# Two attention and mixture-of-experts layers: layer-norm statistics spread over attention steps, token normalisation on GpSimd, three more batches masked by TensorE

## What is computed

```python
x = x + attn_a(LN(x))   # 16 heads of 8, causal mask, softmax(q k / sqrt(8))
x = x + ffn(LN(x))      # top 2 of 8 experts per token, silu(x Wg) * (x Wu) @ Wd
x = x + attn_b(LN(x))   # 16 heads of 8, no mask, per-head shift and scale from norms of q, k and x
x = x + ffn(LN(x))      # the same weights as the first ffn
```

## Time and profile before

| | |
|---|---|
| median of three runs | 1166.69 us (1163.05 to 1168.38) |
| the profiled execution's own time, and its span | 1166.68 us, 1164.9 us |
| TensorE matmul, weight load | 1029.9 us busy (88%), 716.6 us (62%) |
| VectorE | 755.5 us (65%) |
| ScalarE | 672.4 us (58%) |
| GpSimd | 525.5 us (45%) |
| chain that ended last | TensorE 60%, VectorE 11%, issue 6%, GpSimd 5%, DMA 4% |
| granted TensorE clock over the span | 0.92 |

### The profile page before, as it was taken

How to read it: one execution, slowest core, us unless ns; L and a number is a source line. 1 busy time by engine, 2 the same in 40 slices (tenths; PEclk the granted TensorE clock), 3 DMA queues, 4 the chain that set the end, 5 groups by cost and what they waited for, 6 DMA issues and landing times.

```text
span 1164.9 us, 28879 instructions
## 1 busy us (share of the span) xinstructions
PE 1029.9 (88%) x9290; PEld 716.6 (62%) x9290; DVE 755.5 (65%) x2322; ACT 672.4 (58%) x1399; POOL 525.5 (45%) x980
## 2 busy tenths in 40 slices
PE   2998999897989999999798979999888799999990
PEld 1444555453468989999443434444443589999990
DVE  4687778877777333456777888888877663334442
ACT  2365676663644545556277858897757445455550
POOL 2243444332742610344687736455736436004455
PEclk9998999996989999999778979998888899999995
DMA  6446544562235878887544323343221469778873
GB/s 152 104 114 138 116 110 99 151 181 57 54 118 174 271 233 236 260 255 236 125 111 104 101 56 85 89 107 84 65 49 44 130 191 280 227 242 256 272 225 109
DMA packets 201723, 175.03 MB, mean 150 GB/s; under 512 B 19812, under 2 KB 160616, under 8 KB 201576
## 3 DMA queue, kind: packets, MB, share of 16 engines
q1 hardware_dynamic: 193384, 156.41, 49.1%
q0 software_dynamic: 8192, 16.79, 4.8%
HBM read 122.99 MB, written 50.14 MB: 149 GB/s over the span
## 4 chain that ended last, share of the span: by engine, by line
PE 60%; DVE 11%; issue 6%; POOL 5%; DMA 4%; SPq 3%; ACT 1%; POOLq 0%; ACTq 0%; DVEq 0%
PE psS L1358 9%; PE psT L1365 9%; PE psO L321 8%; PE psS L355 7%; PE psO L1381 4%; PE psN L1381 4%; DVE mx L671 4%; PE psS L386 3%; PE psT L363 3%; POOL xn L1259 3%; PE psM L276 2%; PE psN L328 2%; DMA eo<-ysb 2%; PE psN L337 1%; PE psM L1346 1%
## 5 line engine op out<-in xcount | busy, mean ns | idle before, releaser
L671 DVE TENSOR_REDUCE mx<-psS 128x3 f32<-128x384 f32 (+1 forms) x512 | 311.4, 617 | 119.5 <-PE psS L386 61.8
L355 PE MATMUL psS<-kst,qst 48*128 48x256 bf16 (+1 forms) x1024 | 201.7, 286 | 46.4 <-DVE mx L671 33.2
L558 ACT ACTIVATE pT<-psT,scb 128x512 f32<-128x512 f32 x256 | 193.9, 777 | 43.2 <-PE psT L363 40.7
L363 PE MATMUL psT<-qst,kst 50*128 50x256 bf16 (+1 forms) x1024 | 194.7, 278 | 4.6 <-DMA qst<-scr_m 2.2
L1422 DVE TENSOR_TENSOR hT<-sg,psT 128x512 f32<-128x512 f32 x142 | 97.5, 686 | 154.4 <-PE psT L1365 127.7
L1245 POOL DMA_INDIRECT xg<-xn,slot x128 | 123.1, 962 | 131.3 <-DVE ysb L1417 72.1
L1358 PE MATMUL psS<-xTt,wgc 128*128 128x128 f32 x1136 | 153.7, 279 | 5.7 <-issue 5.3
L355 PEld LDWEIGHTS psS<-kst,qst 48*128 48x128 bf16 x1024 | 66.2, 97 | 146.0 <-DVE mx L671 68.2
L1365 PE MATMUL psT<-xTt,wuc 128*128 128x128 f32 x1136 | 152.2, 278 | 1.5 <-DMA wuc<-in_L_ffn_Wu 1.4
L790 POOL TENSOR_SCALAR_AFFINE_SELECT pT<-pT 128x256 f32<-128x256 f32 x224 | 90.6, 412 | 133.0 <-ACT pT L553 131.8
L553 ACT ACTIVATE pT<-psT 128x384 f32<-128x384 f32 x256 | 122.9, 490 | 46.1 <-PE psT L363 35.9
(11 more groups left out here) (225 smaller groups left out, 1595.1 us busy)
## 6 DMA issues: line engine op xcount, KB each, us to landing
wgc<-in_L_ffn_Wg SPq DMA_DIRECT2D x142, 256.0 KB, 3.1
wuc<-in_L_ffn_Wu SPq DMA_DIRECT2D x142, 256.0 KB
scr_part<-part SPq DMA_DIRECT2D x128, 128.0 KB, 2.1
qst<-scr_part SPq DMA_DIRECT2D x64, 192.0 KB, 3.7
kst<-scr_part SPq DMA_DIRECT2D x64, 192.0 KB, 4.7
xin<-xg SPq DMA_DIRECT2D x142, 64.0 KB
eo<-ysb SPq DMA_DIRECT2D x142, 64.0 KB
scr_part<-part SPq DMA_DIRECT2D x32, 192.0 KB, 1.9
```

The source lines that it names most:

```text
L355: return nc.tensor.matmul(ps[:, c0:c0 + n], q_[r64, t, q0], k_[r64, t, 0:n], start=(half == 0), stop=True, skip_group_check=True)
L363: return nc.tensor.matmul(ps[:, c0:c0 + T - q0], k_[m64, t, half * P:half * P + P], q_[m64, t, q0:T], start=(half == 0 or not L.causal), s ...
L558: nc.scalar.activation(pT[:, g % 8, 0:cols], psT[g % 2][:, 0:cols], ACT.Exp, scale=scb[r][:, 0, i:i + 1], bias=scb[r][:, 1, i:i + 1]).then ...
L671: nc.vector.tensor_reduce(mx3[:, u, 0:n, pos:pos + 1].rearrange("p a b -> p (a b)"), psS[h % 2][:, 0:kcols(L)].rearrange("p (a k) -> p a k ...
```

## The change

`MASKED` goes from 14 to 11: batches 11, 12 and 13 (steps 14, 15, 16) are masked by TensorE too. `ffn_over` loses the wait for the stores. In A's step 14 GpSimd normalises block h-1 behind each head h-1 of its loop (the hook's h is 1 to 16), and the calls of `dve_tokens` there are gone. The statistics of 16 blocks begin a step earlier, with a pair of bn_stats at every second head, and are aggregated and rooted at heads 0, 1 and 2 of the next: steps 4 and 5, and 12 and 13 of A, 13 and 14 of B. Those of B's blocks 16 to 31 are split into two halves of 8 blocks, with a pair at every fourth head of step 6 (9) and the rest at heads 0 to 2 of step 7 (10). The combine at (7, 2) moves to (8, 4).

```diff
--- before.py
+++ after.py
@@ -38,7 +38,7 @@
 MINUS_ONES = struct.unpack("<f", bytes([0x80, 0xBF, 0x80, 0xBF]))[0]
 DEPTH_SCALE = float(12.0 ** -0.5)
 PCH = 23
-MASKED = B - 2
+MASKED = B - 5
 
 POS = [8 * (h // 8) + 4 * (h % 2) + (h % 8) // 2 for h in range(H)]
 RING = 3
@@ -899,8 +899,6 @@
         def ffn_over(eng, l):
 
             eng.wait_ge(f_sem["y"], TILES * (l + 1))
-            for i in range(2):
-                eng.wait_ge(f_st[i], tiles_done(i, l, TILES))
 
         LG_COPIES = (0, 1, 3, 4)
 
@@ -1498,6 +1496,12 @@
                     lo, hi = {0: (0, 2), 1: (2, 4), H: (4, 7)}[h]
                     for pair in range(7 * (j - 2) + lo, min(7 * (j - 2) + hi, 2 * SIZE[1])):
                         pool_gather(pool, 1, pair)
+                if l == 0 and j == 14 and h > 0:
+                    k = h - 1
+                    if k == 0:
+                        pool.wait_ge(s_ln[0], 1)
+                    nc.gpsimd.tensor_scalar(xn[:, k, :], x[:, k, :], mean_rstd[:, k, 0:1], mean_rstd[:, k, 1:2],
+                                            ALU.subtract, ALU.mult).then_inc(r_sem["xn"], 1)
                 if l == 0 and (j, h) in FIRST_SCATTERS:
                     pair = FIRST_SCATTERS.index((j, h))
                     if pair == 0:
@@ -1638,10 +1642,12 @@
                     dve.wait_ge(s_xrest, 16)
                     dve_ln_stats(dve, 4, HALF, s_lnA)
                     dve.wait_ge(s_lnA, 2)
-                if l == 0 and j == 5 and h == 0:
+                if l == 0 and j == 4 and h == 0:
                     dve.wait_ge(s_xlast, 16)
-                if l == 0 and j == 5:
-                    dve_ln_at(dve, h, HALF, HALF, s_lnA, 3)
+                if l == 0 and j == 4 and h % 2 == 0:
+                    dve_ln_at(dve, h // 2, HALF, HALF, s_lnA, 3)
+                if l == 0 and j == 5 and h < 3:
+                    dve_ln_at(dve, HALF // 2 + h, HALF, HALF, s_lnA, 3)
                 if l == 0 and j == 1 and h == 15:
                     dve.wait_ge(s_mset, 2 * RING)
                     nc.vector.memset(half[0:1, 0, :], -0.5).then_inc(s_half, 1)
@@ -1649,19 +1655,22 @@
                     dve.wait_ge(s_cst, 16)
                     nc.vector.memset(onesb[:], 1.0).then_inc(s_half, 1)
                     nc.vector.tensor_copy(triu[:], cst[:, CST_TRIU:CST_TRIU + P]).then_inc(s_half, 1)
-                if l == 1 and (j, h) in ((4, 4), (5, 4), (6, 4), (7, 2)):
-                    dve_combine_1(dve, 0, j - 4)
+                if l == 1 and (j, h) in ((4, 4), (5, 4), (6, 4), (8, 4)):
+                    dve_combine_1(dve, 0, min(j - 4, 3))
                 if l == 1 and (j, h) == (2, 12):
                     dve_route_part(dve, 1, 2)
-                if l == 1 and j == 7:
-                    dve_ln_at(dve, h, SIZE[0], SIZE[1], s_lnB, 3)
-                if l == 0 and j == 13:
-                    if h == 0:
-                        dve.wait_ge(x1, HALF)
-                    dve_ln_at(dve, h, 0, HALF, s_ln[0], 1)
-                if l == 0 and j == 14:
-                    if h % 4 == 1:
-                        dve_tokens(dve, 0, h - 1, h + 3)
+                for part, (first, times) in enumerate(((6, 3), (9, 4))):
+                    lo, count = SIZE[0] + part * SIZE[1] // 2, SIZE[1] // 2
+                    if l == 1 and j == first and h % 4 == 0:
+                        dve_ln_at(dve, h // 4, lo, count, s_lnB, times)
+                    if l == 1 and j == first + 1 and h < 3:
+                        dve_ln_at(dve, count // 2 + h, lo, count, s_lnB, times)
+                if l == 0 and j == 12 and h == 0:
+                    dve.wait_ge(x1, HALF)
+                if l == 0 and j == 12 and h % 2 == 0:
+                    dve_ln_at(dve, h // 2, 0, HALF, s_ln[0], 1)
+                if l == 0 and j == 13 and h < 3:
+                    dve_ln_at(dve, HALF // 2 + h, 0, HALF, s_ln[0], 1)
                 if l == 0 and j == 15:
                     if h == 9:
                         dve_logits(dve, 0, 0, QUADS[0], 1)
@@ -1671,10 +1680,12 @@
                         dve_counts(dve, 0)
                 if l == 0 and j == 16 and h < 4:
                     dve_route_part(dve, 0, h + 4)
-                if l == 1 and j == 14:
-                    if h == 0:
-                        dve.wait_ge(x1, SIZE[0])
-                    dve_ln_at(dve, h, 0, SIZE[0], s_ln[2], 1)
+                if l == 1 and j == 13 and h == 0:
+                    dve.wait_ge(x1, SIZE[0])
+                if l == 1 and j == 13 and h % 2 == 0:
+                    dve_ln_at(dve, h // 2, 0, SIZE[0], s_ln[2], 1)
+                if l == 1 and j == 14 and h < 3:
+                    dve_ln_at(dve, SIZE[0] // 2 + h, 0, SIZE[0], s_ln[2], 1)
                 if l == 1 and j == 16 and h in (8, 9):
                     if h == 8:
                         dve_logits(dve, n, 0, QUADS[0], LG_COPIES[n] + 1)
```

## The result

**Slower: 1174.53 us, median of 8 runs (1170.17 to 1177.75), against 1163.82 (8 runs, 1161.44 to 1168.38) of the kernel before; the ratio is 1.0087, with an interval of 1.0065 to 1.0109.** The forecast was 1164.7 us and no change. The profiled execution of the kernel after took 1173.72 us, its span is 1171.9.

The account below looks back on a forecast made before the run. TensorE was taken to bound plain attention steps, VectorE having 3.3 (A) and 2.7 us (B) to spare. The terms summed to -1.95 us against the profiled 1166.68, giving 1164.7 us, range 1156 to 1172.

Parts of the forecast that it names:

- The clock behind each root: After each of five statistics roots in A and B: one short stretch at half clock, 1.7 us lost; bounds 0 and 5.1.
- A, steps 4 to 6: -1.65: Attention A, statistics dealt out: 7.1 us over plain steps becomes 5.45 (pairs 0.3, hole 3.45, clock 1.7), so -1.65 us.
- A, steps 12 to 14: -1.85: Attention A, statistics dealt out: 7.3 us over plain, without TensorE's own transposing, becomes 5.45, so -1.85 us.
- The root's place is dearer: Root at heads 0 to 2: TensorE's scores of head 5 wait 3.45 us for head 3's reduction, where 2.7 was before.
- Step 14 "near 18.3": Attention A: listed as a sign that the forecast is right, step 14 near 18.3 us, 18.9 before.
- B, steps 6 to 10: +1.6: Attention B: 12.3 us over plain becomes 13.9, with two roots of 5.1 each and a combine of 3.1, so +1.6 us.
- B, steps 13 and 14: -1.8: Attention B: 8.6 us over plain becomes 6.8, of which pairs 1.0 (0.5 to 3), so -1.8 us.
- Masks: +3.6: Causal masks on TensorE in A's steps 14, 15, 16 cost 1.0, 1.1, 1.5 us: +3.6; bounds 0 and 7.2.
- Tokens: 0: Group 0's 16 tokens on GpSimd in A's step 14, where it loses 16 masks: no cost, 0 us.
- Stores' wait: -1.85: End of feed-forward 0: without the wait for the last stores, B's first scores follow VectorE's copy; -1.85 us (0 to -1.9).
- The rival of dearer roots: Five roots at heads 2 to 5, each followed by 10.2 us at half clock, 3.4 more each: 1181.7 us; chance 0.19.

Follow-up runs that it names:

- after_dealt: The kernel after with each root's 13 instructions dealt one to a head, heads 2 to 14; 0.9980 of the kernel before, 1221.14 us.
- best: The kernel before without the stores' wait, with the change's statistics placement, roots dealt one instruction to a head, xg's fills in steps 9 to 12; 0.9917, 1155.27 us.
- late_root: The kernel after with aggregation and root at heads 8, 9 and 10 instead of 0, 1 and 2; 1.0043 of the kernel before, 1168.63 us.
- zero_early: The kernel after with xg's eight zero fills moved from steps 13 and 14 to steps 9 to 12; 1.0074 of the kernel before, 1232.19 us.
- zero_before: The kernel before with xg's zero fills moved to steps 9 to 12, alone; 1.0027 of the kernel before, 1166.02 us.
- best_tokens: The kernel best with group 0's 16 tokens on GpSimd in step 14, masks as before; 0.9990 of the kernel before.
- ffn: The kernel before without the wait of TensorE and ScalarE for feed-forward 0's last stores, alone; 0.9986 of the kernel before, 1219.99 us.
- dealt: The kernel before without the stores' wait, with the change's statistics placement and roots dealt one instruction to a head; masks and tokens as before; 0.9951, 1218.05 us.
- masks: The kernel before with MASKED = B - 5 alone; 1.0055 of the kernel before, 1230.91 us against 1221.89 on a slower chip.

## Why the prediction was wrong

The prediction summed to -1.95 us; 10.7 came.

- **The clock behind each root: this is where it failed.** The step is "I take 1.7, one short stretch as in step 5, because there is now one root to a step with nothing else bunched round it". That is 3.4 us at half clock a root, 17 in all. It held in A's step 5. Step 13 of A has 10.2 us and steps 7, 10 and 14 of B 6.8 each, 34.1 with step 5: up to 17.1 us of loss where 8.5 were put down. So the term was mis-sized by up to 1.7 us a root on average. The reason given did not hold: the last pair of the step before reaches into the root's step, and in step 13 a fall of 3.4 us follows its wait of 0.84, ahead of the 6.8 at the root's own hole. With the roots dealt out the five steps keep 0 to 3.4 us each (after_dealt, best), so about that much belongs to what stands beside the root. By the Trainium skill, TensorE: Matmul & The Clock Gate, Part 1, it is idleness that sets the throttle; the trace agrees in kind, since the fall at 220.3 lies in a wait of 2.51 us. Which waits bring a fall and how long it is, the runs leave open (last section).
- **"A, steps 4 to 6: -1.65" and "A, steps 12 to 14: -1.85".** They measured +0.05 and +4.0 us in the trace (54.85 against 54.80; 60.15 against 56.16). In steps 12 to 14 the long fall is up to 3.4 us of the miss and the wait in step 14, below, 2.15; the hole was 0.9 shorter than forecast. In steps 4 to 6 the clock term was right, but step 6 stays 1.1 us over plain: it has a wait of 1.01 us for the maxima's load that stood there before too (0.91) and had been counted to the statistics. The pairs were put at 0.3 us on their step and cost 0.7 (steps 4 and 12 are 16.6 where they were 15.9).
- **"The root's place is dearer", a hole of 3.45 us.** The conclusion was right and its mechanism wrong. The hole measured 2.51 us, no deeper than the 2.69 of before and the 2.68 of late_root. By late_root the place costs about 0.4% all the same; what its trace shows of it is the wait in step 14.
- **Step 14 "near 18.3".** It was 20.7. The prediction put nothing on it: where the stalls of step 13 went it did not ask what had stood in their shelter, which was the spacing of SyncE's zero fills and stores. The wait of 2.15 us behind them is most of the 2.4 us missed; zero_early takes it away (step 14: 18.4), and zero_before shows that before the change there was nothing to take.
- **"B, steps 6 to 10: +1.6"** measured +1.0 (104.23 against 103.24), with steps 7, 8 and 10 at 22.9, 19.9 and 23.0 for the forecast 22.7, 20.7 and 22.7. The lengths are right, and that is luck in part: the hole was 2.5 us for 3.45 and the time at half 6.8 us for 3.4, which nearly cancel. The combine was put at 3.1 us and costs 2.3 alone (step 8), the pairs of step 9 at 0.2 and cost 0.9. The 3.1 of step 6 may have held GpSimd's pace too, which was not tried: its additions of x and the bias come every 20.4 to 20.9 us through steps 2 to 6 in both kernels, so when step 3 is short (17.95) step 4 waits (23.04).
- **"B, steps 13 and 14: -1.8"** measured +0.3. Step 14 was forecast near 23.4 and is 23.41, again with a shorter hole (2.14) and twice the time at half (6.8). Step 13 was put at 1.0 us over plain and is 3.1: 1.5 are the pairs and 1.6 go with a fall of 3.4 us, since the same step is 19.0 us, at full clock, in the eight other kernels with these pairs that show no fall in it. The upper bound (3) was the value.
- **"Masks: +3.6".** Step 15 grew by 2.0 us and step 16 by 0.7, for 1.1 and 1.5 forecast, but in the second trace of the same kernel the two are no longer than before; in step 14 the cost can't be told apart from the wait. The ratios give 0.2 to 0.6%, with 3.6 us (0.3%) inside.
- **"Tokens: 0".** Right for the change, and for the reason given, that the masks leave. One weight load of the transposes waited 0.4 us for them. best_tokens shows what it costs if the masks stay: 2 us in step 14. The exclusion of the two engines that the Trainium skill gives (SBUF — State Buffer, Who interferes with whom) stayed as small as before: the two of VectorE's split instructions that start among GpSimd's tokens in the kernel after take 0.67 and 0.68 us, and the tokens a median of 0.79, one of them 1.36.
- **"Stores' wait: -1.85".** 1.6 us came in the trace, and 1.7 by ffn's ratio, which does not tell it from 0. Steps 2 to 6 of B are 0.8 us longer than before, so part may be given back, as ffn's rival had it. The first scores of B follow the last copy at once:

```profile
570.62 0.28 DVE L1415 COPY ysb<-psN 128x128 f32<-128x128 f32 x1
```
```profile
570.95 0.40 PE L355 MATMUL psS<-kst,qst 48*128 48x256 bf16 x4 [1.92 <-DVE ysb L1415]
```

The copy ends at 570.90, the scores start 0.05 us later, where they started 1.9 us later.

The rival of dearer roots is what happened, from one of its two sources: it decided from 1.6 us more a root, and the clock took up to 1.7 more on average, while the hole, its other source, was shorter. Its price at full (1181.7) was too high, because only step 13 of A has the fall of 10.2 us; B's three roots have 6.8 and A's step 5 has 3.4. The block as a whole, hole and clock, is worth 2.6 us in each of the five places by after_dealt. Last, the sum stood against a profiled execution 2.9 us slower than the median of the eight runs: the forecast of 1164.7 was in truth a forecast of no gain at all.

## What to carry to other kernels

A chain of small dependent instructions on an engine that feeds the bound one costs more than its own length when it is issued as a block: here a block of 2.9 us brought a wait of 2.5 and 3.4 to 10.2 us at half clock. Dealing its 13 instructions over 13 heads took away more (1.2%) than any other part of this change was worth, and the kernel with roots dealt and the new placement is the first that beats the kernel before. When a stall or a slow stretch is removed, ask of each transfer behind it when it would be ready if the engine came on time, and where a long transfer is issued ahead of a short one in the same queue. Moving that transfer elsewhere can move the wait along with it. And work moved off an engine may be the room that another part of the same change needs: price such parts together.

## What the runs showed of the hardware

**A small store behind a big fill is late.** From the issue of the 8-KB store of the maxima to the load that waits for it, 3.41 us passed in the kernel after, 1.2 us behind a 576-KB fill; 2.20 in the kernel before, 1.5 us behind one; 1.75 in late_root, 1.9 us behind; and 1.32 in best, where no fill is near (1.3 to 2.0 in all traces without one):

```profile
236.80 0.30 SPq L830 DMA_DIRECT2D scr_m<-mrow  x1
238.12 0.54 SPq L833 DMA_DIRECT2D qst<-scr_m  x2
```

Near fills some issues also hold SyncE longer, up to 1.26 us in the kernel after and 1.39 in late_root; in best those of step 14's stores take 0.35 to 0.50. Fills are not the only cause: zero_before has one of 1.87 us with none near.

**A short wait can be followed by a long stretch at half clock, or by none.** Waits of 0.84 and 2.51 us in step 13 stand beside 10.2 us at 0.50. The same wait of 0.84 us at the same place of late_root's step 13 is followed by no fall, and in best by one of 3.4 us. In step 14 of B best has waits of 1.02 and 0.66 us and keeps its clock at 1.00; dealt has the same two and 3.4 us at half behind them. Waits of 1.8 to 3.8 us behind a root's block stand beside falls of 3.4 to 13.7 us in every trace. What decides was not settled.

**Chips, or one chip at two times, differ beside GpSimd's indirect DMAs.** Plain steps are the same to 0.02 us on both kinds of chip (15.88 for A, 17.55 for B). Step 17 of A, in which GpSimd issues scatters, is 15.73 us in the kernel after and was 19.54 in masks, at the same clock of 1.00 and with TensorE's work about the same:

```profile
303.16:322.70 19.54, 16.04 (x184) 8.09 (x184) 10.57 (x27) 9.79 (x22) 10.56 (x11) 1.00 0.13 40
```

Step 17 of B, near its end, goes from 20 to 26 us, steps 2 to 6 of B, where GpSimd gathers, from 80 us to between 86 and 93. Some 36 of the 53 us between the traces of the kernel before and of ffn lie in the two feed-forward stretches, which were not looked into. The slower traces have more time at half clock, 230 to 284 us in all against 155 to 193; which is cause and which effect is open. Steps with a root at the old place are even shorter there (27.6 and 24.8 us for steps 7 and 14 of B, 29.1 and 26.2 on the faster chip). It need not be the chip: the third and the fourth group of runs, at 1163.9 and 1227.3 us, carry the same chip number. An execution that is 5% longer on another chip is no sign of a change; only the kernel before, run beside it, is the measure. Why these transfers are slower there was not tried.
